# Storing the attention result x2 from GpSimd by row scatters

## What is computed

```python
x = x + xattn(layernorm(x), ctx, ctx, wq, bq, wk, bk, wv, bv, wo, bo)   # 16 heads of 16
x = x + ffn(layernorm(x), Wg, ln_scale, ln_bias, W1, b1, W2, b2)        # 8 experts, hidden 64, exact gelu
```

## Time and profile before

| | |
|---|---|
| median of 3 runs | 1676.08 us (1675.87 to 1678.66) |
| the profiled execution | 1676.87 us, its span 1674.8 us |
| PE busy | 1532.9 us, 92% of the span |
| DVE busy | 1226.1 us, 73% |
| ACT busy | 925.6 us, 55% |
| POOL busy | 425.9 us, 25% |
| attention phase, about | 65 to 1125 us of the span |
| FFN phase, about | 1165 to 1675 us |

### The profile page before, as it was taken

The page is one execution under the profiler, slowest core; times in us unless marked ns, Lnnn a source line. Parts: engine busy times, 40 slices in busy tenths (PEclk is TensorE's granted clock), DMA queues, the critical chain, the costliest instruction groups (busy, mean ns, idle before and its releaser), DMA issues.

```text
span 1674.8 us, 40310 instructions
## 1 busy us (share of the span) xinstructions
PE 1532.9 (92%) x15566; PEld 1225.3 (73%) x15566; DVE 1226.1 (73%) x2878; ACT 925.6 (55%) x1578; POOL 425.9 (25%) x599
## 2 busy tenths in 40 slices
PE   6599999999999999999999999967999999999998
PEld 4477777777777777777777777855777777777776
DVE  4777777777777777777777777755777777777775
ACT  3276667667766776667666766643333423333342
POOL 3122222222322232232222222212223232322321
PEclk8699999999999999999999999997999999999999
DMA  4454456445644554555455545511121212212121
GB/s 120 109 156 137 127 147 165 135 128 148 166 133 132 151 163 128 140 151 156 128 149 151 155 125 148 138 56 45 57 76 51 76 57 71 72 55 76 51 76 38
DMA packets 148385, 190.36 MB, mean 114 GB/s; under 512 B 15531, under 2 KB 99046, under 8 KB 148198
## 3 DMA queue, kind: packets, MB, share of 16 engines
q1 hardware_dynamic: 148198, 187.79, 40.3%
HBM read 52.48 MB, written 33.55 MB: 51 GB/s over the span
## 4 chain that ended last, share of the span: by engine, by line
PE 72%; DVE 17%; issue 5%; ACT 5%; DMA 1%; SPq 0%; POOL 0%; ACTq 0%; DVEq 0%
PE s_ps L495 12%; PE st_ps L513 11%; PE pp_ps L1148 8%; DVE negmax L893 7%; PE pv_ps L1094 6%; PE s_ps L1051 6%; PE pp_ps L1156 5%; PE pp_ps L1121 4%; PE st_ps L1079 3%; PE pv_ps L1102 3%; PE t_ps L1070 2%; PE pp_ps L461 2%; PE s_ps L502 2%; PE t_ps L1062 2%; PE pp_ps L1142 2%
## 5 line engine op out<-in xcount | busy, mean ns | idle before, releaser
L893 DVE TENSOR_REDUCE negmax<-s_ps 128x8 f32<-128x1024 f32 x256 | 313.3, 1224 | 144.7 <-PE s_ps L1051 137.4
L788 ACT ACTIVATE pT<-st_ps 128x1024 f32<-128x1024 f32 x256 | 263.1, 1028 | 99.8 <-PE st_ps L1079 99.2
L513 PE MATMUL st_ps<-w_hi,q_packed 128*128 128x256 f32 x1024 | 213.5, 293 | 0.7 <-DVE q_packed L415 0.7
L701 POOL TENSOR_TENSOR q_parts<-q,q_parts 128x1024 bf16<-128x1024 f32 x32 | 68.3, 2134 | 537.5 <-ACT q_parts L782 537.5
L1094 PE MATMUL pv_ps<-pT,v 128*32 128x128 f32 x4096 | 166.4, 278 | 27.7 <-DVE attn L909 18.9
L495 PE MATMUL s_ps<-k_packed,w_hi 128*128 128x512 f32 x512 | 173.9, 421 | 18.0 <-ACT pT L324 18.0
L513 PEld LDWEIGHTS st_ps<-w_hi,q_packed 128*128 128x128 f32 x1024 | 168.0, 188 | 10.5 <-issue 6.4
L318 ACT ACTIVATE offhotT<-pv_ps 96x512 bf16<-96x512 bf16 x32 | 19.0, 593 | 257.5 <-PE pv_ps L482 257.5
L1079 PE MATMUL st_ps<-q_packed,k_packed 98*128 98x128 bf16 x2048 | 157.9, 220 | 3.4 <-DMA q_packed<-negmaxT 2.0
L1051 PE MATMUL s_ps<-k_packed,q_packed 96*128 96x128 bf16 x2048 | 158.4, 220 | 2.0 <-DVE negmax L893 1.3
L1051 PEld LDWEIGHTS s_ps<-k_packed,q_packed 96*128 96x128 bf16 x2048 | 128.2, 98 | 24.6 <-issue 20.9
(11 more groups left out here) (164 smaller groups left out, 3646.5 us busy)
## 6 DMA issues: line engine op xcount, KB each, us to landing
q_packed<-q_parts SPq DMA_DIRECT2D x192, 256.0 KB, 3.8
k_packed<-k_parts SPq DMA_DIRECT2D x192, 256.0 KB, 4.2
xin<-in_x_dram SPq DMA_DIRECT2D x32, 512.0 KB, 3.7
cin<-in_ctx_dram SPq DMA_DIRECT2D x32, 512.0 KB, 3.6
x_scratch<-xb SPq DMA_DIRECT2D x32, 512.0 KB, 5.2
xin<-x_scratch SPq DMA_DIRECT2D x32, 512.0 KB, 4.7
out_dram<-xb SPq DMA_DIRECT2D x32, 512.0 KB, 3.2
q_packed<-negmaxT SPq DMA_DIRECT2D x256, 4.0 KB
```

Of the source, the lines that this page charges most:

```text
L513: t.matmul(o, h[n % 2][:, m, tok].bitcast(F32R), w[:, m, :].bitcast(F32R), start=(m == 0 and k == 0), stop=False)
L701: g.tensor_tensor(parts[z][:, 2, :, :], z32[z][:], parts[z][:, 1, :, :], ALU.subtract).then_inc(s_lo, 1)
L788: a.activation(pT[u % 2][:], st_ps[:], ACT.Exp, scale=DH ** -0.5).then_inc(s_exp, 1)
L893: v.tensor_reduce(negmax[u % 2][:], s_ps[:].rearrange("p (h s) -> p h s", s=P), AX_X, ALU.max, negate=True).then_inc(s_red, 1)
```

## The change

The store of x2 moves from SP to POOL. In place of one DMA of 512 KB for a group, POOL issues four indirect DMAs, one for each of the four sequences; each scatters 128 rows of 1 KB from `xb` to rows of `x2_scratch`, whose numbers come from a small table `row_of` (128x4, `row_of[p, b] = 128 b + p`), which POOL fills once at the start; the group is chosen by a constant element offset. Each of the four adds 16 to `st_x2`, so all waits on `st_x2` count four times as much. In POOL's `group(n)` the store of group n - 1 stands between `lo(n + 1, 0)` and `norm(n + 2)`. The store of the last group stands behind the FFN's `norm(1)`, ahead of `lo_of_xT(0)`.

```diff
--- before.py
+++ after.py
@@ -59,6 +59,7 @@
 
     x2_dram = nc.dram_tensor("x2_scratch", [BATCH, T, D], F32, kind="Internal").ap()
     x2_v = x2_dram.rearrange("(g b) t d -> g t b d", b=GB)
+    x2_rows = x2_dram.rearrange("a t d -> (a t) d")
 
     with ExitStack() as stack:
         def sb(name, shape, dt=F32):
@@ -112,6 +113,7 @@
         packed = [[sb(f"{z}_packed{n}", [P, H, GT], BF16) for n in range(2)] for z in "qk"]
 
         v1 = [sb(f"v{n}", [P, GB, H, HP]) for n in range(2)]
+        row_of = sb("row_of", [P, GB], mybir.dt.uint32)
         xb = [sb(f"xb{n}", [P, GB, D]) for n in range(2)]
         negmax = [sb(f"negmax{n}", [P, HC]) for n in range(2)]
         negmax_p = [sb(f"negmax_p{n}", [P, 2 * HC], BF16) for n in range(2)]
@@ -184,6 +186,7 @@
         s_bn, s_mv, s_ve, s_nm, s_rstd, s_shift, s_xn, s_xb = (sem(n) for n in (
             "bn_stats_done", "mean_var_done", "var_eps_done", "neg_mean_done", "rstd_done", "shift_done", "xn_done",
             "xb_done"))
+        s_row = sem("row_numbers_done")
         ld_mx = [sem(f"max_rows_loaded{n}") for n in range(2)]
         s_tl = sem("transposed_lo_done")
         s_pp, s_pe = sem("projection_in_psum"), sem("projection_kept")
@@ -266,7 +269,7 @@
             for n in range(2):
                 sp.wait_ge(f_st[n], 8 * GROUPS)
 
-        def ffn_pool(pool):
+        def ffn_pool(pool, store_x2):
             g = nc.gpsimd
 
             def norm(n):
@@ -294,6 +297,7 @@
 
             norm(0)
             norm(1)
+            store_x2(LAST)
             lo_of_xT(0)
 
             def group(n):
@@ -332,7 +336,7 @@
             for c in range(C):
                 keep_xT(0, c)
 
-            act.wait_ge(st_x2[0], 8 * GROUPS)
+            act.wait_ge(st_x2[0], 8 * GB * GROUPS)
             copy(0)
 
             def group(n):
@@ -344,7 +348,7 @@
                         a.copy(onehotT[n % 2][:], onehotT_ps)
                     if m == 1 and n < LAST:
                         if n == 0:
-                            act.wait_ge(st_x2[1], 8 * GROUPS)
+                            act.wait_ge(st_x2[1], 8 * GB * GROUPS)
                         copy(n + 1)
                 if n < LAST:
                     for c in range(C):
@@ -564,10 +568,6 @@
                 wait(sp, s_pp, at(ITEMS, g - 1, 4))
                 sp.dma_start(cin[:], c_v[g]).then_inc(ld_c, 16)
 
-            def store_x2(g):
-                dst = x2_v[g]
-                wait(sp, s_x2, at(GB, g, GB))
-                sp.dma_start(dst, xb[g % 2][:]).then_inc(st_x2[g % 2], 16)
 
             def pack(g, z, part):
                 if part == 0:
@@ -631,8 +631,6 @@
                 if g < LAST:
                     pack(g + 1, 0, 2)
                     pack(g + 1, 1, 0)
-                if g > 0:
-                    store_x2(g - 1)
                 if later(g, 3, 2):
                     load_max(*later(g, 3, 2))
                 if g < LAST:
@@ -655,11 +653,10 @@
 
             for n in range(2):
                 sp.wait_ge(s_xb, GROUPS - 1 + n)
-                sp.wait_ge(st_x2[n], 16)
+                sp.wait_ge(st_x2[n], 16 * GB)
                 ffn_load(sp, n)
-            store_x2(LAST)
             for n in range(2):
-                sp.wait_ge(st_x2[n], 8 * GROUPS)
+                sp.wait_ge(st_x2[n], 8 * GB * GROUPS)
             ffn_sync(sp)
 
 
@@ -704,11 +701,20 @@
 
                 pool.wait_ge(s_xn, at(GB, n, GB))
 
-                wait(pool, st_x2[n % 2], (n // 2) * 16)
+                wait(pool, st_x2[n % 2], (n // 2) * 16 * GB)
                 for b in range(GB):
                     last = g.tensor_tensor(xb[n % 2][:, b, :], xin[n % 2][:, b, :], bo_all[:], ALU.add)
                 last.then_inc(s_xb, 1)
 
+            def store_x2(n):
+
+                wait(pool, s_x2, at(GB, n, GB))
+                for b in range(GB):
+                    g.indirect_dma_start(x2_rows, bass.IndirectOffsetOnAxis(ap=row_of[:, b:b + 1], axis=0),
+                                         xb[n % 2][:, b, :], None,
+                                         element_offset=n * GT * D).then_inc(st_x2[n % 2], 16)
+
+            g.iota(row_of[:], [[T, GB]], base=0, channel_multiplier=1).then_inc(s_row, 1)
             norm(0)
             pool.wait_ge(s_bo, 1)
             residual(0)
@@ -716,9 +722,13 @@
             for z in range(2):
                 lo(0, z)
 
+            pool.wait_ge(s_row, 1)
+
             def group(n):
                 if n < LAST:
                     lo(n + 1, 0)
+                if n > 0:
+                    store_x2(n - 1)
                 if n + 2 <= LAST:
                     norm(n + 2)
                 if n < LAST:
@@ -727,7 +737,7 @@
 
             for n in range(GROUPS):
                 group(n)
-            ffn_pool(pool)
+            ffn_pool(pool, store_x2)
 
 
         @block.scalar
```

## The result

The changed kernel takes 1786.95 us (median of 4 runs, 1784.85 to 1788.05) against 1676.77 us (1675.87 to 1678.66, 4 runs) for the kernel before beside it: a ratio of 1.0654, 95% interval 1.0636 to 1.0673, 110 us or 6.5% slower. The forecast said slower, 1707 us with a range of 1670 to 1785. The direction was right, the size was missed by 80 us, and the range was missed by 2.

What follows compares the result with a forecast made beforehand. PE was taken as the bound. The profiled 1676.87 us + 34.8 (late shift) - 4 (SP's queue) + 0.2 (passage) = 1707.9, or 1707 against the median; range 1670 to 1785 us for 8 in 10.

Steps and rivals of the forecast that it cites:

- the two slacks: Attention phase: ACT's normalisation waiting for POOL's shift, and SP's last copy of packed k before PE's scores, decide the cost.
- S: POOL's time for one indirect DMA, taken as 1.3 us between bounds of 0.36 and 2.14 us; four make 5.2 us.
- The first limb: POOL's norm behind the scatters gives ACT the shift late: 4S - 4.0 = 1.2 us a group, 34.8 us in 29 groups.
- Where the 5.2 us go: Step following the scatters' time on POOL through the norm and third part of k to later engines; holds both limbs.
- The second limb: POOL's third part of k ends later, before SP's copy and PE's scores; binds from 4S = 5.3 alone, adds nothing.
- The 4 us of gain: SP loses one store issue a group, so PE's 0.15 us wait for maxima in unit 5 goes in 27 groups.
- The passage and the start: Passage to the FFN: PE loses 0.1 to 0.2 us waiting for turned x; filling the table at the start costs nothing.
- Rival (a): Scatters fit on POOL, S up to 1.0: 1673 us, or 1655 if additions end before DVE's small steps; 22 in 100.
- Rival (b): Scatters hold up DVE's small steps in unit 3, 0.65 us a group, adding 20 us: 1728 us; 15 in 100.
- Rival (c): POOL far slower at scatters, S over 1.7, row numbers collected one by one: 1777 us at S = 1.9; 18 in 100.
- Rival (d): Queue never the matter: maxima land as late as before, only the 4 us go; inside the forecast's range, no own chance.

Runs made afterwards that it cites:

- clearings: The kernel before with six memsets of an unused tile on POOL at the scatters' place, no DMA from POOL: 1724.32 us, ratio 1.0287.
- the run with later additions: Changed kernel with each scatter issued alone, and POOL's additions held back until the last unit's scores are there: 1682.22 us, 1.0043 against the kernel before.

## Why the prediction was wrong, point by point

- **The bound now, and which slacks decide**: PE as the bound and POOL without a share of the chain hold after as before. That the two slacks decide does not.
- **S, 1.3 us each, 5.2 us in all**: measured 5.15 us in all, from 0.98 us of work and 0.30 us between two. The estimate of four words a row for 128 rows (1.4 us) was right by luck: 16 rows cost 0.86 us, 128 cost 0.98, so an indirect DMA is nearly all fixed cost here, and the nearest row was the power of four elements, 1.02 us. The 1.3 us hold only with the 0.30 us between two counted in.
- **The first limb, 29 x (4S - 4.0)**: right as a mechanism and near as a price, with clearings (48.4 us measured for 49 computed, of it some 13 us by the lower clock, which it didn't have). In the changed kernel it costs nothing: ACT doesn't wait for POOL, since it is later itself by more than POOL is. The forecast wrote that it would be wrong in this case whatever the time, and so it is. This is the step that failed: "Where the 5.2 us go" looked only for those who take POOL's results, and took it that PE's signals reach ACT and DVE as before. In their place the trace shows ACT and DVE waiting for PE, 77 us in all in 30 groups, and TensorE's clock at 0.58 for 4 us behind that.
- **The second limb** (part of k): adds nothing, as said. Scatters moved behind it cost more, not less.
- **The 4 us of gain**: wrong. The wait went, and nothing came back; it was hidden. The 27 waits sum to 8.0 us on the weight loads and, on PE's matmuls, to 2.0 us in 7, so that 27 x 0.15 took one group's wait for all.
- **The passage and the start**: DVE's addition ends at 1254.71 and POOL's part of the turned x starts at 1259.93, 5.2 us later; PE's next product waits till 1261.26, which is 0.4 us later than the row of before moved by 110 us. The forecast had 0.1 to 0.2.
- **Rival (a), fits**: refuted by S. But its mechanism, additions that end before DVE's small steps, is real: it is what makes one scatter at a time faster than the kernel before. The forecast priced it at 18 us; the run with later additions measures 11, ends of the phase included.
- **Rival (b), DVE held by scatters**: the small steps under the scatters take 0.17 us at 523.91 and 524.12. It is nothing. The Trainium skill, "SBUF — State Buffer", section "Who interferes with whom", infers that descriptor making needs only the shared write side; this trace agrees with it.
- **Rival (c), POOL far slower**: the time was near its 1777 us, for another reason.
- **Rival (d)**: the gain on the queue is absent, so it was right in its small part. The Trainium skill, "DMA: Bandwidth & Descriptors", section "Issuing engines are not separate DMA queues", says that issuing elsewhere saves only the sequencer's time; the run with SP's store later (1.0018) and the one with plain transfers (1.0070), neither of them faster, agree with it.

What the loss of 110 us is made of, by the group shown: 2.9 us of late signals of PE, 1.5 us at the low clock behind them, 0.6 us back from the collision that is now hidden.

Open is through what the scatters and PE touch each other. Shown is that it takes indirect DMAs in flight on POOL and dense short matmuls on PE, and that both PE's signals and its own next instructions come late. The instruction queues of the page read alike before and after (q8: 127 packets, 2.08 MB, 0.5%), which gives no sign of slower instruction loading but doesn't rule it out. That the delay sits with semaphores was not tried.

## What to carry to other kernels

A DMA with addresses in a table is not a plain DMA issued elsewhere: price it in time on GpSimd (1.28 us each in a row here) and also ask what TensorE does meanwhile, since beside dense short matmuls its results reached the others late. If such DMAs are needed, try to issue each as soon as its own data is ready, apart from the next: the same 128 scatters cost 110 us in fours and were 5 us better than the plain store one at a time. And when a moved step frees or shifts a neighbour, look for a collision that it undoes: the additions' place was worth more here than the store's queue.

## What the runs showed of the hardware that was not expected

- Signals of TensorE reach ScalarE and VectorE up to 3.1 us late in the group shown while GpSimd runs four indirect DMAs in a row; the hold could be made in the FFN phase with matmuls of 32 rows by 128 columns beside them, and not with either alone. Beside plain DMAs of GpSimd, or clearings of 5.69 us, no wait on "remote" shows.
- An indirect DMA takes GpSimd on average 0.98 us for 128 rows, with 64 bytes or 1 KB a row, and 0.86 us for 16 rows of 64 bytes; a plain DMA of 128 KB takes it 0.56 us.
- After a hold with TensorE busy for 5.16 of 8 us, its granted clock was 0.58 over the next 4 us, and the 256-column matmuls took 0.41 us in place of 0.28.
